# A decoder block on one core: ScalarE, not TensorE, writes the mask ahead of each second score pass, in a new order of the turn

## The reference

```python
x = x + delta_rule_mixer(layernorm(x), ...)         # chunked delta rule, FIR filters, gates
x = x + cross_attention(layernorm(x), ctx, mask, ...)
x = x + quantised_ffn(layernorm(x), ...)
# cross attention, 16 batches, 16 heads of 16 columns, 256 queries x 256 keys:
scores = einsum('bhqd,bhkd->bhqk', Q, K) / sqrt(16)
scores = where(mask == 0, -inf, scores)
out = einsum('bhqk,bhkd->bhqd', softmax(scores), V)
```

## Time and profile before

| what | value |
|---|---|
| median of 3 runs | 1300.8 us (1296.5 to 1303.19) |
| the profiled execution's own time | 1304.4 us |
| its span, first to last instruction | 1302.6 us |
| TensorE busy | 1073.4 us, 82% of the span |
| VectorE busy | 984.7 us, 76% |
| ScalarE busy | 755.2 us, 58% |
| GpSimd busy | 637.6 us, 49% |
| mean granted TensorE clock | 0.912 |

### The profile page before, as it was taken

How to read it: one execution, slowest core, us unless ns; L and a number is a source line. 1 busy time by engine, 2 the same in 40 slices (tenths; PEclk the granted TensorE clock), 3 DMA queues, 4 the chain that set the end, 5 groups by cost and what they waited for, 6 DMA issues and landing times. The chain is left out here.

```text
span 1302.6 us, 27987 instructions
## 1 busy us (share of the span) xinstructions
PE 1073.4 (82%) x8553; PEld 801.0 (61%) x8626; DVE 984.7 (76%) x2955; ACT 755.2 (58%) x1456; POOL 637.6 (49%) x2360
## 2 busy tenths in 40 slices
PE   5889888675677789999999999999999877775756
PEld 4677677674565656776676677677677645433224
DVE  4898989677666867877887787787788667734985
ACT  5778878332343356656666665665665543444866
POOL 4777775304275355466556546546545643111007
PEclk9988988885576889999999999999999988997989
DMA  6666666454215233434334343343342331204006
GB/s 186 202 203 219 204 196 199 169 114 144 75 55 138 74 99 107 130 95 138 103 122 125 110 135 104 108 145 115 111 130 77 114 111 54 66 33 176 10 1 227
DMA packets 159829, 160.31 MB, mean 123 GB/s; under 512 B 65320, under 2 KB 126656, under 8 KB 159680
## 3 DMA queue, kind: packets, MB, share of 16 engines
q1 hardware_dynamic: 155552, 157.47, 39.9%
q10 hardware_dynamic: 4128, 1.05, 0.4%
HBM read 96.34 MB, written 61.87 MB: 121 GB/s over the span
## 5 line engine op out<-in xcount | busy, mean ns | idle before, releaser
L2142 DVE CUSTOM_DVE_ANT_0 x_psA<-x_psA,x_mask_q 128x256 f32<-128x256 f32 x496 | 201.1, 447 | 74.0 <-PE x_psA L1431 73.8
L1694 ACT ACTIVATE x_PT<-x_psB 128x512 f32<-128x512 f32 x240 | 143.6, 598 | 159.3 <-PE x_psB L1458 157.1
L314 DVE SCALAR_TENSOR_TENSOR a_conv<-a_ps_proj,taps,a_conv 128x253 f32<-128x253 f32 (+2 forms) x288 | 115.0, 471 | 15.0 <-ACT a_conv L381 15.0
L537 PE MATMUL a_ps_proj<-a_hT,wqkv 128*128 128x256 f32 x384 | 106.8, 427 | 9.9 <-DVE a_conv L314 6.6
L1431 PE MATMUL x_psA<-x_Ks,x_Qs 96*128 96x256 bf16 x496 | 97.3, 278 | 16.1 <-DVE x_maxima L2142 15.7
L1458 PE MATMUL x_psB<-x_Qs,x_Ks 98*128 98x256 bf16 x480 | 93.3, 275 | 7.8 <-issue 6.2
L537 PEld LDWEIGHTS a_ps_proj<-a_hT,wqkv 128*128 128x128 f32 x384 | 79.1, 217 | 29.6 <-issue 14.6
L1860 POOL TENSOR_SCALAR x_parts_q<-x_rest 128x512 bf16<-128x512 f32 x16 | 23.9, 1496 | 118.2 <-DVE x_rest L2114 118.2
L1455 PE MATMUL x_psB<-x_mask_k,x_ident_bf 128*128 128x512 bf16 x170 | 66.3, 390 | 11.5 <-ACT x_PT L1694 9.4
L1472 PE MATMUL x_psO<-x_PT,x_V 128*32 128x256 f32 x1024 | 70.9, 396 | 1.6 <-ACT x_PT L1694 1.6
L2142 DVE DVE_READ_ACCUMULATOR2_ANT x_maxima<- 128x1 f32 x512 | 72.1, 141 | 0.0
(11 more groups left out here) (383 smaller groups left out, 3225.9 us busy)
## 6 DMA issues: line engine op xcount, KB each, us to landing
scratch_keypack<-a_keypack SPq DMA_DIRECT2D x16, 768.0 KB, 3.7
c_keypack<-scratch_keypack SPq DMA_DIRECT2D x16, 768.0 KB, 4.7
x_Ks<-scratch_k_parts SPq DMA_DIRECT2D x192, 64.0 KB, 2.2
matrix<-scratch_taps_copies SPq DMA_DIRECT2D x32, 256.0 KB, 4.0
scratch_k_parts<-x_parts_k SPq DMA_DIRECT2D x32, 192.0 KB, 2.3
scratch_q_parts<-x_parts_q SPq DMA_DIRECT2D x32, 192.0 KB, 2.3
x_Qs<-scratch_q_parts SPq DMA_DIRECT2D x32, 192.0 KB, 2.9
a_x_in<-in_x SPq DMA_DIRECT2D x16, 256.0 KB, 3.7
```

The lines of the kernel that those rows point to most:

```text
L314: nc.vector.scalar_tensor_tensor(acc, ps_proj[PROJ_BANK[p]][:, c, 0:L - j], taps[:, p, c, TAPS - 1 - j:TAPS - j], acc, ALU.mult, ALU.add). ...
L537: last = nc.tensor.matmul(ps_proj[PROJ_BANK[p]][:, o], wqkv[:, p, c, o * P:(o + 1) * P], hT[par][:, c], start=c == 0, stop=c == FC - 1)
L1694: nc.scalar.activation(PT[:, k % (2 * GROUP)], bank_B(b, k)[0], ACT.Exp, scale=XD ** -0.5).then_inc(pexp_ready, 1)
L2142: last = nc.vector.tensor_tensor_reduce(bank_A(b, k)[0][:, s], bank_A(b, k)[0][:, s], mask_q[:, t], 1.0, LOWEST, ALU.add, ALU.max, maxima[ ...
```

## The change

`MASKED_BY_ACT` becomes the heads 1 to 15. For batches 0 to 13, `kB{k}` on ScalarE waits for its own exponential of head k-1 (`pexp_ready`), copies the transposed mask (`mask_k`, bf16 in SBUF, 128 x 512) into bank psB (fp32 in PSUM), and `sB{k}` on TensorE waits for `mask_written` and issues its two matmuls of scores alone. Head 0 of each batch, and all heads of batches 14 and 15, keep the identity matmul.

`C_ORDER` is a new list: 15 entries more, and the others in another order. The stages of 25 operations differ. Those of the DMAs (`ld_*`, `st_kp`, `st_qp`) and of `qlow`, `ostat`, `stats`, `gelu2`, `vc`, `pv3`, `OT1`, `sums3a`, `inve` rise by one or two while their places on their engines move toward the head, and `sq0`, `sq1`, `mA1`, `h3`, `h3m` fall by one while they move toward the end, so in time they stand near where they stood. The diff, with the old list cut to its ends:

```diff
-C_ORDER = [(0, "tt"), (3, "og2"), (3, "oge"), (1, "rv"), (3, "ogs"), (3, "ctxT"), (2, "tT"), (2, "tTc"), (3, "cTc"),
...
-           (5, "OT1"), (3, "Q0st"), (0, "sums3a"), (3, "vproj"), (3, "vc"), (3, "sA0"), (0, "inve"), (3, "mA0")]
+C_ORDER = [(3, "gelu2"), (4, "vc"), (1, "xur"), (3, "oge"), (6, "OT1"), (4, "sA1"), (6, "pv3"), (1, "p2"), (3, "og2"),
+           (4, "sA2"), (5, "sB0"), (2, "tT"), (3, "ctxT"), (2, "gate1"), (4, "sA3"), (6, "tu0"), (1, "a0"), (4, "sA4"),
+           (5, "sB1"), (6, "tu1"), (3, "kproj"), (6, "tuo"), (4, "sA5"), (5, "sB2"), (3, "to"), (6, "wop"), (5, "ld_Q0"),
+           (6, "ld_S"), (4, "ld_c"), (4, "ld_x"), (5, "ld_Q1"), (3, "ld_hT"), (5, "ld_K1"), (8, "st_h3"), (1, "ld_vs"),
+           (7, "st_x2"), (0, "ld_pack"), (4, "st_kp"), (4, "st_qp"), (4, "ld_K0"), (2, "tTc"), (5, "eB0"), (5, "kB1"),
+           (3, "cTc"), (2, "gelu1"), (4, "Q1st"), (5, "sB3"), (3, "proj"), (5, "sB4"), (4, "sA6"), (2, "logits"), (7, "tuh"),
+           (5, "sB5"), (3, "ogs"), (4, "mA2"), (1, "sums1"), (1, "sums0a"), (1, "sums3a"), (4, "mA3"), (6, "ot0"),
+           (1, "sums1a"), (6, "ot1"), (4, "mA4"), (0, "invk"), (1, "sums0"), (4, "mA5"), (0, "invx"), (3, "krest"), (6, "x2"),
+           (6, "statb"), (1, "inve"), (3, "x1"), (3, "statx"), (2, "pr1"), (4, "mA6"), (2, "pr2"), (1, "sums3"), (0, "tt"),
+           (0, "invp"), (4, "mA7"), (2, "pr3"), (3, "xnx"), (5, "eB1"), (5, "kB2"), (6, "ofc"), (3, "khigh"), (5, "eB2"),
+           (5, "kB3"), (3, "oTc"), (1, "sqv"), (5, "eB3"), (5, "kB4"), (1, "ua0"), (5, "eB4"), (5, "kB5"), (5, "eB5"),
+           (1, "w0"), (2, "exp"), (5, "kB6"), (1, "uc0"), (5, "eB6"), (1, "S"), (5, "kB7"), (7, "h3c"), (5, "eB7"), (5, "kB8"),
+           (3, "xTc"), (5, "eB8"), (1, "ua1"), (5, "kB9"), (1, "b0"), (4, "sA7"), (1, "c0"), (5, "sB6"), (1, "state"),
+           (5, "pv0"), (4, "K1st"), (1, "r1"), (4, "mA8"), (2, "mixa"), (4, "mA9"), (2, "mixb"), (2, "mixc"), (3, "qrest"),
+           (2, "mix"), (0, "invr"), (4, "mA10"), (2, "osum"), (2, "osum3"), (1, "rhs1"), (5, "sB7"), (4, "sA8"), (3, "xT"),
+           (1, "a1"), (5, "sB8"), (4, "sA9"), (3, "qproj"), (1, "b1"), (5, "sB9"), (4, "sA10"), (1, "c1"), (0, "gram0"),
+           (5, "sB10"), (4, "sA11"), (3, "K0st"), (1, "out"), (5, "sB11"), (4, "sA12"), (0, "gram1"), (5, "pv1"), (4, "mA11"),
+           (0, "invq"), (0, "att0"), (7, "rstdb"), (1, "delta"), (4, "mA12"), (1, "sums2a"), (0, "invb"), (4, "qlow"),
+           (3, "ostat"), (2, "stats"), (1, "rv"), (3, "scale"), (3, "oF"), (3, "klow"), (3, "rstdx"), (0, "att1"), (4, "mA13"),
+           (1, "sums2"), (3, "qhigh"), (1, "w1"), (5, "eB9"), (5, "kB10"), (1, "uc1"), (2, "osq"), (5, "eB10"), (0, "nat0"),
+           (5, "kB11"), (0, "xd"), (5, "eB11"), (5, "kB12"), (0, "nat1"), (1, "sqd"), (5, "eB12"), (5, "kB13"), (5, "OT0"),
+           (5, "eB13"), (5, "sB12"), (4, "sA13"), (0, "p1"), (5, "sB13"), (4, "sA14"), (5, "pv2"), (4, "sA15"), (5, "sB14"),
+           (3, "vproj"), (2, "oT8"), (4, "maxT"), (5, "sB15"), (3, "sA0"), (2, "og1"), (4, "mA14"), (4, "mA15"), (6, "h3"),
+           (0, "invd"), (2, "st8"), (4, "sh2"), (0, "inva"), (3, "mA0"), (6, "h3m"), (0, "invs"), (3, "mA1"), (1, "st16"),
+           (5, "kB14"), (0, "w5"), (5, "eB14"), (0, "sq0"), (5, "kB15"), (2, "oT8c"), (4, "sh1"), (5, "eB15"), (0, "sq1"),
+           (3, "Q0st")]
 
 LOWEST = -3.0e38
-MASKED_BY_ACT = ()
+MASKED_BY_ACT = (1, 2, 3, 4, 5, 6, 7, 8, 9, 10, 11, 12, 13, 14, 15)
```

## The result

The change makes the kernel slower: a median of 1391.48 us (4 runs, 1388.98 to 1395.01) against 1301.07 for the kernel before beside it, a ratio of 1.0702 [1.0665, 1.0739]. The profiled execution took 1388.98 us, its span is 1387.0.

What follows compares the result with a forecast made beforehand. TensorE was taken as the bound in turns 6 to 16, with ScalarE fullest afterwards. Savings of 20.9 us there and 1.6 in turn 5, 22.5 in all, took the 1300.8 median to a forecast of 1278.5 us, range 1262 to 1304.

Steps and rivals of the forecast that it cites:

- What it must wait for: Step walking a turn on ScalarE, TensorE and VectorE: ScalarE stands still 2.5 us, turn 45.0 us; DMAs keep their distance.
- the five: Cases: ScalarE overloaded 0.15, waits eat the gain 0.14, ScalarE hardly waits 0.12, clock falls 0.04, the forecast 0.55.
- TensorE's term: Fifteen identity matmuls dropped at 0.21 us each save 3.2 us a turn; TensorE's load falls from 43.9 to 40.7.
- ScalarE's terms: Added per turn: mask copies 9.0 us, two more table loads 2.6, two terms of 0.6; load 29.7 becomes 42.5.
- the two small ones: ScalarE, per turn: exponentials no longer overlapped, 0.6 us; masks waiting for the engine's own result, 0.6 us, at most 2.4.
- The rule against it: Skill page's drain at table switches on ScalarE: two new switches would cost 5.3 us, making the turn 47.8 us.
- The waits: ScalarE's standing still within a turn, 2.5 us in all, added to its 42.5 us load.
- the five places: ScalarE's stalls: eB5 0.5, uc0 and S 0.5, qhigh 0.5, oT8c 0.4, crowd at the turn's head 0.6 us.
- The fill: Filling turns, 289 to 477.5 us: counted as 0 with 5 us either way; a larger change would mean wrong.
- the two terms that I could price: Filling turns: sq1 waiting for a load holds the solve back some 2 us; a1 comes up to 4.5 us sooner.
- The clock: Turns 6 to 16: granted clock below 1.00 would mean wrong; rival of a falling clock, about 1302 or more, chance 0.04.
- signs of being wrong: Turn of 46.5 us or more, gap around loads, ScalarE idle over 4 us, clock below 1.00, fill changed over 5 us.

Runs made afterwards that it cites:

- e10_pack_behind_shift: Changed kernel with SyncE's stores and loads reordered, last weight loads later, and st_x2 and ld_pack moved behind ld_K1; 1273.7 us, 0.9800 of the kernel before.
- e7_sp_full: Changed kernel with SyncE's key and query stores early, query loads at once, and hT, context and x loads ahead of ld_S; 1299.32 us, ratio 0.9992.
- e1_sp_repaired: Changed kernel with only SyncE's order altered: key and query stores ahead of the bulk loads, query loads right behind their store; 1367.6 us, ratio 1.0509.

## Why the prediction was wrong, point by point

**The step that failed** is the last sentence of "What it must wait for": "From turn to turn, GpSimd's steps and the DMAs keep their distance". The front says of the moved DMAs that "in time they stand near where they stood". I had read that from stages and places in the list. What counts is what stands ahead of each entry in SyncE's own queue: for each DMA, when its data is ready, when SyncE has got past the entries ahead of it, and how many bytes it then lies behind. Walked so, `st_kp` comes free only after `h3c` (21.2 us of waiting) and after the mixer (6.3), and lands in 7.7 us and not in 2.2. The step stood in the sum with nothing; the turn of 45.0 became one of 52.0, with 7.9 us of waiting for the queries in turn 11. The parts by themselves show that this is the whole loss: SyncE's order alone costs 8.7% (in the order of before it is other loads that come late), the change without its masks as much as with them, and mending that one queue takes the ratio from 1.0702 to 0.9992, with the rest of the change in place.

I did name the DMAs as the next to be late, by `st16` and `ld_S`. The right queue, but I gave it no price and no rival, and the entries that came late first were others. The case that came was in none of the five: all of them lay with ScalarE, TensorE and its clock, or `mA` on VectorE.

**TensorE's term**: 3.2 us a turn. Measured by taking the masks away in the mended kernel: the turn is 1.24 us longer and TensorE busy 1.5 longer (43.56 against 42.05). The busy time understates it, since the records of that turn hold 10 of its 16 identity matmuls. The 0.21 us from start to start was right for one of them; how much of the 15 the turn gets back depends on whether TensorE is what the turn waits for, and with ScalarE at 40.3 and VectorE at 37.9 us I take it to be so only in part. TensorE's load after the change was too low in the sum: 40.7 us were said, and it is 42.05 in the mended turn, at the full clock. So TensorE is still the fullest engine there, ahead of ScalarE's 40.3. Its waits are 1.3 us, where I had said 4, most of them for ScalarE.

**ScalarE's terms**: the copy's length and the loads held, the two small ones did not. The groups of turn 11 of the changed kernel:

```profile
L1696 ACT ACTIVATE x_PT<-x_psB 128x512 f32<-128x512 f32 x16 | 9.5, 595 | 1.8 <-PE x_psB L1460 1.6
L1701 ACT ACTIVATE x_psB<-x_mask_k 128x512 f32<-128x512 bf16 x15 | 9.0, 598 | 0.3
L1696 ACT ACT_TABLE_LOAD x2 | 2.6, 1283 | 0.0
```

15 copies of 0.598 us (taken: 0.60) and four loads of 1.283 (two before exponentials, two before gelus, L1620 and L1644). The sum was too high: ScalarE is busy for 40.3 us, not 42.5. Without the masks it has 32.1, which is 2.4 more than the 29.7 of the earlier trace rows (the two loads: 2.6), and with them 8.2 more. That is 0.55 a mask and not 0.68, the 0.60 and the terms for lost overlap and its own result together. The timeline of ScalarE shows why:

```profile
804.72 1.28 ACT L1696 ACT_TABLE_LOAD   x1
806.01 0.60 ACT L1696 ACTIVATE x_PT<-x_psB 128x512 f32<-128x512 f32 x1
806.64 0.60 ACT L1701 ACTIVATE x_psB<-x_mask_k 128x512 f32<-128x512 bf16 x1
807.17 0.58 ACT L1662 ACTIVATE x_cT<-c_ps_gram 128x512 f32<-128x512 f32 x1
807.77 1.28 ACT L1620 ACT_TABLE_LOAD   x1
809.07 0.84 ACT L1620 ACTIVATE c_g<-c_ps_e,c_bg 128x256 f32<-128x256 f32 x2
```

The mask waits 0.03 us for its exponential (taken: 0.04), but the operation behind it starts 0.53 us after it. The overlap that the exponential loses, the mask gains. By the 8.2 us that the 15 masks add, the term "its own result" and the lost overlap cost nothing beyond the plain copy.

The rule against it, the drain of some 1.38 us at every switch (the Trainium skill, ScalarE: Activation LUTs, "What ACT_TABLE_LOAD costs"), has no place in these rows: 0.01 to 0.02 us on either side of a load, at four loads a turn. The same page of the Trainium skill ("Step-by-step") calls PSUM the faster destination; the copy into PSUM takes what a copy out of PSUM takes, 0.598 beside 0.59 of the earlier trace rows, so nothing of it shows here.

**The waits**: I counted 2.5 us of ScalarE's. In the mended kernel the waits of that turn are 1.6 + 0.6 + 0.2 = 2.4, and ScalarE's idle time is 3.6 (43.87 - 40.26). Of the five places that the walk named two came, `eB5` (0.49) and `qhigh` (0.60); the others of the 2.4 us stand at `eB4`, `eB7`, `eB8`, `eB12` and a copy of the solve. So the near sum is partly luck. The walk over three engines gave the right size; it left out the fourth queue.

**The turn**: 45.0 predicted, 45.5 in the nearly undisturbed turn 15 of the changed kernel, 43.9 in the mended one. That it comes so near is partly luck. ScalarE's load was said 2.2 us too high and its idle time 1.1 too low. And I gave the whole gain to the masks and nothing to the order; the order brought 1.8 us of the 3.0 and the masks 1.2.

**The fill**: 9.0 us longer, outside the band of 5. Of the two terms that I could price one was about right: `a1` starts at 311.70 us and not at 315.31, 3.6 sooner (4.5 at most was said). The other was too large: `a0` waits for ScalarE as predicted but starts only 0.4 us later than before (302.92 for 302.54), not 2. In this stretch TensorE waits 11.4 us for the queries' loads, where before it waited for no DMA. With SyncE's order mended (e10_pack_behind_shift) those waits are gone and turn 5 starts at 478.6, 1.1 us later than before, so nearly all of the nine are the queue's as well.

**The clock**: below 1.00 in turns 6 to 16, which I had named as a sign against me. It follows the stall and is no cause of its own: in turn 11 it is 1.00 up to the stall and falls only then; the turn with 9.6 us of idle TensorE has 0.91, the one with 3.4 has 1.00; and turns 6 to 16 of the mended kernel have 0.99 together, where TensorE is busy for 463.0 of 484.8 us.

**The numbers around them.** Turn 17 of the kernel before starts at 1036.28 us, where its load stands, and not at 1038.0; so turn 16 has 45.2 us, the 11 turns a mean of 46.7, and their term is 19.2 us rather than 20.9. The sum itself, 1300.8 - 22.5, gives 1278.3 and not 1278.5, and 7.7 and 5 us around it give 1266 to 1291, not 1268 to 1289. None of this touches the sign. Of the signs of being wrong four came: the turn, the idle time of ScalarE (14.0 us in turn 11), the clock and the fill. No gap stood around the loads.

## What to carry to other kernels

When an order is rewritten, walk every in-order queue, the DMA-issuing engine's first: for each of its entries note when the data is ready, what the entries ahead of it wait for, and the bytes issued just before it. A short store that others need belongs ahead of entries with late inputs and ahead of bulk transfers; moving it and the loads around it off their places cost 7% here, where the best kernel of this document wins 2%. And price "its distance stays the same" like any other term: with a lower bound of nothing and an upper bound of the longest wait that now stands in front of it.

## What the runs showed of the hardware that I had not expected

- A store of 192 KB lands in 2.2 us alone and in 6.7 to 7.7 us behind 2 MB issued in the 4 us before it, from the same queue, in 4.0 behind 1 MB. Even 8 KB of shift rows are held up: 4.0 us to land with `st_x2` and the megabyte of `ld_pack` in front, which costs TensorE 2.2 us in a turn of e7_sp_full, and 1.8 us when those stand elsewhere.
- A stall costs twice. In turn 11 the granted clock is 1.00 before the wait of 7.9 us, 0.68 in it and 0.67 in the 8 us after it, a mean of 0.91, and the same matmuls take 2.5 us longer than in turn 15: 8.7 us for a turn in which TensorE is idle for only 6.2 us more.
- Four such waits stood in one queue (key and query stores; `hT` behind the shift rows; the shift rows behind the bulk; weight loads in front of the query store). The second and the third grew only when the one before was gone (`hT`: 3.5 us over turns 6 to 16 of the changed kernel, 4.2 us in a single turn of e1_sp_repaired), and the first mending, which removed the longest wait of the profile, took the ratio only from 1.0702 to 1.0509.
